# A two-layer transformer block for eight batches: unrolled batches, layer A prepared a batch ahead, the last output units in the turn

## Chip, cores and metric

The kernel runs on one core of one Trainium2 chip. The metric is the device time of one execution in microseconds; times given as the result of a kernel are medians of several executions, times read from a view come from one profiled execution.

## The reference

Eight batches of 512 rows by 128 features go through two layers in float32. `x` is the input.

```python
# layer A, on n = layernorm(x): 16 heads of 8 for q and k, of 32 for v
Q = split_heads(n, 16);  K = split_heads(n @ Wk + bk, 16);  V = split_heads(n @ Wv + bv, 16)
attn = softmax(Q @ K.T + causal mask)
o = (attn @ V) merged to 512 columns
x = x + n + gelu(o) @ Wf + bf
# layer F, on n = layernorm(x): 8 heads of 64, 8 experts for each head
q, k = n @ w_q, n @ w_k;  gates = sigmoid(n @ w_gate)      # (heads, 8)
gm = one_hot(argmax(gates)) * gates
values = einsum('bhne,ehdk,bnd->bhnk', gm, value_experts, n)
out = (softmax(q @ k.T / 8, causal) @ values)
x = x + einsum('bhne,ehkd,bhnk->bhnd', gm, output_experts, out) summed over heads
```

## The kernel before

All batches run through the same program on five engines; each engine's order is written out by hand and semaphores tie them together. `each_batch` (L246) runs `first` (layer A of batch 0), then in a hardware loop seven times `body` (layer F of one batch, then layer A of the next), then `last` (layer F of batch 7). Between them all engines meet (`meet`, L249): each drains, SP clears all semaphores of the batch and lets them go on.

Layer A or F is an `attention` over 4 groups of heads (A: 4 heads each, F: 2), each group in 3 stages of key tiles. For each head a *max unit* makes the scores once for their maxima and softmax denominators (PE `max_unit` L490, DVE `max_unit` L1005, ACT `denominators` L740), `negate` (L1021) makes the offsets, which PE transposes and SP writes as extra rows of the operand by DMA (`maxima_rows`, L323), and a *score unit* makes the scores again with them (PE `score_unit` L518, ACT's exponential L788). POOL cuts the causal triangle (L916) and PE multiplies with the values (`weigh`, L538). Max units of group g + 2 run beside the score units of group g.

Layer A has to be prepared: the transposed, normalised input is split into three bf16 parts for q, and K = n Wk + bk likewise for k (`q_part0` L691, `q_rest` L982, `k_part0` L700 and their neighbours, `transposed` L415, `keys_a` L422). SP writes the parts to DRAM (`parts_to_dram`) and reads them back head by head (`restack_a`, L294), once layer F has let the operands go. All this lies beside layer F's first stages. V is made between F and A: `values_a` on PE (L427, twelve matmuls in banks of `ps_exp`) and on DVE (L1000, with the bias).

Layer F begins with `project_f` (L435): transposes, gates, the projections q and k, then 32 *expert values* (L1190 picks them by the gates). Its result is multiplied with the output experts in 32 *output units*: DVE makes `at` = `osb` * `hots` (L1058), PE adds the product to one bank (`product`, L556). A unit's multiplication waits for the product two before it. `OUTPUTS` (L99) places the 32 units: 8 beside F's last steps, 6 beside A's first max units, 18 beside A's 48 score units. The one-hot rows `hots` come from DRAM by large DMAs on ACT's queue (`repeat_hots`, L722).

I call *turn* what lies between the last score unit of layer A and the expert values of the next layer F: the last `weigh`, `outputs_end` (copy of the sum, transposes, addition, L569, L854, L1061), gelu (L816), `project_back` (L627), the sum `x1` (`first_layer`, L1199), the meeting, then statistics and normalising (L961, L970), transposes, `x_high` (L686) and `x_low` (L976), gates and projections.

Of the kernel before, what the change touches and what calls it, by code (L numbers as in the profile page):

```python
# [11 lines left out]

F32 = mybir.dt.float32
F32R = mybir.dt.float32r
# [26 lines left out]
JUNK = 3  # L41
STEPS = {"A": 4, "F": 3}
# [9 lines left out]
BANK = {("F", "xT", 0): 0, ("F", "gate", 0): 1, ("F", "gmT", 0): 1, ("A", "xT", 0): 0, ("A", "K", 0): 1,  # L52
        ("F", "acc", 0): 1, ("F", "out", 0): 0, ("A", "W", 0): 1}
# [25 lines left out]

def place(phases):  # L80


    at, u = {}, 0
    for phase, steps, first, units in phases:
        at.update({(phase, n): [] for n in range(steps)})
        for m in range(units):
            at[phase, first + m * (steps - first) // units].append(u)
            u += 1
    assert u == T * E
    return at  # L90
# [6 lines left out]


OUTPUTS = place([("F", UNITS["F"], 14, 8), ("pre", STAGES * HG["A"], 0, 6), ("A", UNITS["A"], 0, 18)])  # L99


HOTS_AT = {("F", 1): 0, ("F", 4): 1, ("A", 0): 2, ("A", 4): 3}


def build(nc, x, wk, bk, wv, bv, wf, bf, wq, wkf, wg, ve, oe, ident, consts, out):
    ctx = ExitStack()
    with ctx:
# [3 lines left out]
        sems = []  # L111

        def sem(name):
            sems.append(ctx.enter_context(nc.semaphore(name)))
            return sems[-1]
# [15 lines left out]
        bv_sb = sb("bv_sb", [P, S])  # L131
# [6 lines left out]
        x1 = sb("x1", [P, T, D])  # L138
# [31 lines left out]
        raw = {"wq": at[:, 0], "wkf": at[:, 1], "wg": xn["F"][:, 0, 0:64]}  # L170

        rest = pt[:, 7]

        def part(n):

            return pt[:, (2, 3, 6)[n // 2], :].bitcast(BF16)[:, (n % 2) * S:(n % 2) * S + S]
# [5 lines left out]
        def bank(name):  # L182
# [4 lines left out]
        ps_m = [bank("ps_m0"), bank("ps_m1")] + ps_exp  # L187
# [7 lines left out]

        hot_d = nc.dram_tensor("hot_d", (64, S), BF16).ap()
# [6 lines left out]
        cleared = {n: sem(f"cleared_{n}") for n in ("sp", "pe", "act", "pool", "dve")}  # L203
        y_out = sem("y_out")
        first_of_batch = len(sems)
        arrived = sem("arrived")
        x_in = sem("x_in")
        K2 = lambda n: {k: sem(f"{n}{k}") for k in "AF"}
        ln_st, ln_mv, ln_ve, ln_rs, ln_xn = (K2(n) for n in ("ln_st", "ln_mv", "ln_ve", "ln_rs", "ln_xn"))
        xt_ready, xh_done, xl_done = K2("xt_ready"), K2("xh_done"), K2("xl_done")  # L210
        restacked = sem("restacked")
        restacked_a = [sem(f"restacked_a{g}") for g in range(GROUPS)]
        pair_sent = [sem("pair_sent0"), sem("pair_sent1")]
        max_ready, max_done = K2("max_ready"), K2("max_done")
        neg_step, neg_ready = K2("neg_step"), K2("neg_ready")
        t_ready, t_done = K2("t_ready"), K2("t_done")
        mrow = {k: [sem(f"mrow{k}{n}") for n in range(2)] for k in "AF"}
        s_ready, exp_done = K2("s_ready"), K2("exp_done")
        causal, pv_done = K2("causal"), K2("pv_done")
        den_done, ln_done = K2("den_done"), K2("ln_done")  # L220
        sums_out = K2("sums_out")
        q1, q_r, q2, q3 = sem("q1"), sem("q_r"), sem("q2"), sem("q3")
        k_ready, kf, k1, k_r, k2, k3 = (sem(n) for n in ("k_ready", "kf", "k1", "k_r", "k2", "k3"))
        parts_out = sem("parts_out")
        v_ready, va = sem("v_ready"), sem("va")
        resid = sem("resid")
        gelu_done, w_ready, x1_done = sem("gelu_done"), sem("w_ready"), sem("x1_done")
        gate_ready, gate_exp, gate_step, gt_ready, gmt_done = (
            sem(n) for n in ("gate_ready", "gate_exp", "gate_step", "gt_ready", "gmt_done"))
        gt_made = sem("gt_made")  # L230
        zmax_made, zabs_made, low_gate, soft_made, lng_made = (
            sem(n) for n in ("zmax_made", "zabs_made", "low_gate", "soft_made", "lng_made"))
        qk_ready, qk_hi, qk_lo = sem("qk_ready"), sem("qk_hi"), sem("qk_lo")
# [1053 lines left out]
```

## Time and profile before

| | us |
|---|---|
| median of 3 executions | 1541.37 (1540.88 to 1544.47) |
| profiled execution | 1543.4, of which the span is 1541.3 |
| mean granted clock of TensorE | 0.900 of 2.4 GHz |
| PE busy | 1215.5 us, 79% |
| DVE busy | 907.6 us, 59% |
| ACT busy | 895.6 us, 58% |

The chain that ended last has 41% on PE, 24% on ACT, 14% on DVE and 12% in which an engine waited for nothing that the profile shows. Batch after batch is alike: the sum `x1` (L1204) comes at 129.3, 309.9, 493.2, 677.3 us and so on, every 184 us, and last at 1414.5; the rest, layer F of the last batch, takes 126 us. A busy share of the whole span mixes stages with different limits, so the views below are of single stages of one batch.

### The profile page before, as it was taken

Reading aid. Unit: us, or ns where it says so; the run is one execution under the profiler, and the core shown is the slowest. Engines: PE = TensorE matmul, PEld = TensorE weight load, DVE = VectorE, ACT = ScalarE, POOL = GpSimd, SP = SyncE. Lnnn points to the kernel's source line nnn. Section 1 sums busy time; section 2 is a strip of 40 time slices with the busy share of each in tenths; the row PEclk is TensorE's granted clock in tenths of the full one; section 3 lists DMA queues with packets and bytes.
Section 4 is the critical chain, followed back from the end, with each engine's and each line's share of the span. In section 5 each row is a group of like instructions: output and inputs, shape, how many; then the busy total and the mean of one; then the engine's idle time right before and its main releaser. Section 6 shows DMA issues by size and latency. Waiting matters only on the chain.

```text
span 1541.3 us, 19742 instructions
## 1 busy us (share of the span) xinstructions
PE 1215.5 (79%) x5720; PEld 678.2 (44%) x5720; DVE 907.6 (59%) x2786; ACT 895.6 (58%) x2551; POOL 209.9 (14%) x264
## 2 busy tenths in 40 slices
PE   2667888878886879869789688886888778887978
PEld 1114643356433654337443464335643356434643
DVE  5534747367482756728476474745748276572845
ACT  1773567727594366934678246772668527594351
POOL 2020111201111011110112011120110111111010
PEclk9976989979898889979799798997989979898999
DMA  3312631146220651207421164113632055120722
GB/s 89 102 56 49 148 101 44 36 96 143 74 56 17 132 128 44 56 16 165 107 59 29 42 148 111 47 30 82 140 88 65 8 119 136 57 56 9 162 60 61
DMA packets 64163, 122.18 MB, mean 79 GB/s; under 512 B 13971, under 2 KB 29715, under 8 KB 59683
## 3 DMA queue, kind: packets, MB, share of 16 engines
q1 hardware_dynamic: 58950, 87.77, 23.7%
q10 hardware_dynamic: 5120, 33.56, 9.4%
q14 instruction: 82, 0.67, 0.2%
q8 instruction: 11, 0.18, 0.0%
HBM read 61.37 MB, written 9.06 MB: 46 GB/s over the span
## 4 chain that ended last, share of the span: by engine, by line
PE 41%; ACT 24%; DVE 14%; issue 12%; DMA 3%; SPq 3%; POOL 1%; ACTq 1%; POOLq 1%; DVEq 0%
ACT masked L747 11%; PE ps_m L559 8%; ACT pt L788 7%; PE ps_o L552 6%; DVE masked L1016 4%; PE ps_m L403 4%; PE ps_exp L481 3%; PE ps_m L405 3%; PE ps_m L404 3%; PE ps_m L636 3%; DMA s1q<-zeros_d 3%; PE ps_exp L480 2%; PE ps_exp L482 2%; PE ps_max L480 2%; DVE pt L1168 2%
## 5 line engine op out<-in xcount | busy, mean ns | idle before, releaser
L1016 DVE CUSTOM_DVE_ANT_0 masked<-ps_max,mask 128x512 f32<-128x512 f32 (+3 forms) x768 | 352.0, 485 | 228.8 <-PE ps_max L480 152.2
L747 ACT ACTIVATE masked<-masked,low 128x512 f32<-128x512 f32 (+3 forms) x768 | 427.6, 560 | 76.7 <-DVE low L1016 74.3
L788 ACT ACTIVATE pt<-ps_exp 128x384 f32<-128x384 f32 (+1 forms) x576 | 293.7, 523 | 188.3 <-PE ps_exp L482 134.5
L559 PE MATMUL ps_m<-at,oe_sb 128*128 128x512 f32 x512 | 268.6, 611 | 5.6 <-DVE at L1058 3.5
L916 POOL TENSOR_SCALAR_AFFINE_SELECT pt<-pt 128x512 f32<-128x512 f32 (+2 forms) x192 | 133.3, 694 | 800.0 <-ACT pt L788 800.0
L1058 DVE TENSOR_TENSOR at<-osb,hots 128x512 f32<-128x512 f32 x256 | 180.7, 708 | 75.7 <-PE ps_m L559 75.7
L552 PE MATMUL ps_o<-pt,val 128*32 128x128 f32 (+6 forms) x1536 | 191.1, 473 | 11.2 <-POOL pt L916 11.2
L480 PE MATMUL ps_exp<-s1q,s2k 96*128 96x128 bf16 (+3 forms) x512 | 133.5, 319 | 64.6 <-ACT pt L788 53.1
L480 PE MATMUL ps_max<-s2k,s1q 96*128 96x512 bf16 (+3 forms) x512 | 141.4, 326 | 52.6 <-DMA s1q<-zeros_d 39.5
L747 ACT ACTIVATION_READ_ACCUMULATOR masked<-masked,low 128x1 f32 x768 | 151.5, 197 | 0.0
L480 PEld LDWEIGHTS ps_exp<-s1q,s2k 96*128 96x128 bf16 x512 | 43.2, 99 | 226.3 <-ACT pt L788 174.3
L481 PE MATMUL ps_exp<-s1q,s1k 128*128 128x256 f32 (+2 forms) x256 | 108.9, 436 | 34.9 <-DMA s2q<-mt_f 19.0
L480 PEld LDWEIGHTS ps_max<-s2k,s1q 96*128 96x128 bf16 x512 | 49.6, 101 | 133.2 <-issue 48.0
L1190 DVE COPY_PREDICATED val<-osb,ps_exp 128x512 f32<-128x512 uint32 x128 | 92.7, 734 | 19.8 <-PE ps_exp L405 19.8
L559 PEld LDWEIGHTS ps_m<-at,oe_sb 128*128 128x128 f32 x512 | 86.5, 193 | 39.9 <-DVE at L1058 33.1
L481 PEld LDWEIGHTS ps_exp<-s1q,s1k 128*128 128x128 f32 x256 | 54.1, 211 | 89.8 <-issue 54.2
L552 PEld LDWEIGHTS ps_o<-pt,val 128*32 128x32 f32 (+1 forms) x1536 | 54.5, 123 | 88.8 <-issue 55.6
L482 PE MATMUL ps_exp<-s2q,s2k 96*128 96x256 f32 (+2 forms) x256 | 89.5, 360 | 0.0
L481 PE MATMUL ps_max<-s1k,s1q 128*128 128x256 f32 (+2 forms) x256 | 87.2, 350 | 2.8 <-DVE low L1016 2.8
L482 PE MATMUL ps_max<-s2k,s2q 96*128 96x256 f32 (+2 forms) x256 | 85.3, 342 | 0.0
L836 ACT ACTIVATE pt<-ps_m 128x512 fp32r<-128x512 f32 x64 | 38.3, 598 | 75.5 <-PE ps_m L405 74.7
L924 POOL TENSOR_TENSOR val<-val,gmax 128x512 f32<-128x512 f32 x32 | 32.7, 1043 | 334.3 <-DVE val L1190 334.3
(144 smaller groups left out, 1679.9 us busy)
## 6 DMA issues: line engine op xcount, KB each, us to landing
hots<-hot_d ACTq DMA_DIRECT2D x64, 512.0 KB, 5.6
s1q<-pt SPq DMA_DIRECT2D x128, 128.0 KB, 2.4
s1k<-pt SPq DMA_DIRECT2D x128, 128.0 KB, 2.4
s2k<-parts_k SPq DMA_DIRECT2D x96, 96.0 KB
s1q<-parts_q SPq DMA_DIRECT2D x96, 96.0 KB
s2q<-pt SPq DMA_DIRECT2D x64, 128.0 KB, 2.4
s2k<-pt SPq DMA_DIRECT2D x64, 128.0 KB, 2.4
parts_q<-pt SPq DMA_DIRECT2D x24, 128.0 KB, 2.4
```

The source lines that it names most:

```text
L403: mm(dst, lh, rh, start=True, stop=False)
L480: return mm(dst, l1[0:KROWS, h, l2], r1[0:KROWS, h, r2], start=True, stop=True)
L481: mm(dst, l1[0][:, h, l2], r1[0][:, h, r2], start=True, stop=False)
L482: return mm(dst, l1[1][0:KROWS, h, l2], r1[1][0:KROWS, h, r2], start=False, stop=True)
L552: last = mm(ps_o[g % 2][j * w:j * w + w, qt * P:S], val[:, kt, h * w:h * w + w], pt[:, (n % 2) * 4 + j, c0:c1], start=kt == 0, stop=kt == 3)
L559: mm(ps_m[1][:], oe_sb[:, u], at[:, u % 2], start=u == 0, stop=u == T * E - 1).then_inc(at_used, 1)
L747: last = nc.scalar.activation(e, e, ACT.Exp, bias=low[:, g % 2, c:c + 1], scale=-1.0, accum_out=den[:, g % 2, c:c + 1])
L788: nc.scalar.activation(pt[:, (n % 2) * 4 + j, 0:c1 - c0], ps_exp[u % 2][:, c0:c1], ACT.Exp).then_inc(exp_done[k], 1)
L916: nc.gpsimd.affine_select(out=v, in_=v, compare_op=ALU.is_ge, fill=0.0, base=0, pattern=[[0, HG[k]], [0, m], [1, P]], channel_multiplier=- ...
L1016: last = v.tensor_tensor_reduce(out=masked[:, u % JUNK, c0:c0 + w], in0=src[:, c0:c0 + w], in1=mask[:, S - w:S], scale=-1.0, scalar=POS, o ...
L1058: v.tensor_tensor(at[:, u % 2], osb[:, u // E], hots[:, u // E % 2, u % E], ALU.mult).then_inc(at_done, 1)
L1190: v.copy_predicated(val[:, t].rearrange("p (h k) -> p h k", k=64), pick, ps_m[BANK[("F", "moe1", n)]][:].rearrange("p (h k) -> p h k", k=6 ...
```

## The change

1. Semaphores are no longer cleared. Each has a count per batch (`Tally`), waits are for `per * batch + n`, and `for b in range(B)` is unrolled in Python: no meetings, no hardware loop.
2. Layer A of batch b + 1 is prepared in the second half of layer A of batch b (`PREP`: steps 24 to 37), no longer beside layer F. Its V is made in the turn, copied by ACT, written to DRAM (`v_d`) by SP, and read back after layer F. The bias of V moves to the copy of the weighed sums and to gelu.
3. `TURN = 8`: 8 of the 32 output units leave layer A's score steps and stand in the turn. Layer A's other 10 stand in its first 36 steps. The units' multiplication is on VectorE, as before.
4. Some tiles change place: the gates, the transposed output and `project_back` have banks of `ps_max`, the parts lie in `masked`, `x1` and the residual have two buffers, gelu writes the last group to a tile of its own.

```diff
-OUTPUTS = place([("F", UNITS["F"], 14, 8), ("pre", STAGES * HG["A"], 0, 6), ("A", UNITS["A"], 0, 18)])
+TURN = E
+OUTPUTS = place([("F", UNITS["F"], 14, 8), ("pre", STAGES * HG["A"], 0, 6), ("A", 3 * STAGES * HG["A"], 0, 10)])
+PREP = {"stats": 24, "norm": 26, "xT": 28, "q0": 29, "q_rest": 30, "q1": 31, "q2": 32, "K": 32, "k0": 34, "k_rest": 35,
+        "k1": 36, "k2": 37}
...
# SP
+            def layer_a(a):
+                if a + 1 < B:
+                    sp.wait_ge(resid.sem, resid.count(a, 2))
+                    sp.dma_start(x_sb[:], x[a + 1].rearrange("(t p) d -> p t d", p=P)).then_inc(x_in.sem, 16)
+                for g in range(GROUPS):
+                    maxima_rows("A", a, g)
...
+                if a + 1 < B:
+                    parts_to_dram(a + 1, "q")
+                    parts_to_dram(a + 1, "k")
+                    for t in range(T):
+                        sp.wait_ge(va.sem, va.count(a + 1, t + 1))
+                        sp.dma_start(v_d[t], val[:, t]).then_inc(v_out[t].sem, 16)
...
+            def layer_f(f):
+                restack_f(f)
+                for g in range(3):
+                    maxima_rows("F", f, g)
...
+                for g in range(GROUPS):
+                    if g == 2:
+                        maxima_rows("F", f, 3)
+
+                    sp.wait_ge(s_ready["F"].sem, s_ready["F"].count(f, (g + 1) * STAGES * HG["F"]))
+                    restack_a(g)
+                sp.wait_ge(pv_done["F"].sem, pv_done["F"].count(f, NST))
+                for t in range(T):
+                    sp.wait_ge(v_out[t].sem, v_out[t].count(f, 16))
+                    sp.dma_start(val[:, t], v_d[t]).then_inc(v_back.sem, 16)
...
# PE
+            def turn(a):
+
+                f, first = a - 1, T * E - TURN
+                if a + 1 < B:
+                    pe.wait_ge(exp_done["A"].sem, exp_done["A"].count(a, UNITS["A"]))
+                    values_a(a + 1, (0, 1))
+                if f >= 0:
+                    product(f, first - 1)
+                    product(f, first)
+                project_back(a, (0, 1, 2))
+                if f >= 0:
+                    product(f, first + 1)
+                    product(f, first + 2)
+                project_back(a, (3,))
+                if a + 1 < B:
+                    values_a(a + 1, (2, 3))
+                if f >= 0:
+                    for u in range(first + 3, T * E - 1):
+                        product(f, u)
+                transposed("F", a)
+                if f >= 0:
+                    product(f, T * E - 1)
...
+                if n == 0 and k == "A" and b > 0:
+                    if v_back.count(b - 1, 16 * T):
+                        pe.wait_ge(v_back.sem, v_back.count(b - 1, 16 * T))
...
# ACT
+            def turn(a):
+
+                g = GROUPS - 1
+                act.wait_ge(sums_out["A"].sem, sums_out["A"].count(a, g))
+                nc.scalar.activation(osb[:, 0:g], osb[:, 0:g], ACT.Gelu).then_inc(gelu_done.sem, 1)
+                if a + 1 < B:
+                    values_a(a + 1, (0, 1))
+                act.wait_ge(pv_done["A"].sem, pv_done["A"].count(a, NST))
+                if a + 1 < B:
+                    act.wait_ge(parts_out.sem, parts_out.count(a + 1, 16 * WRITES))
+                for t in range(T):
+                    c = slice(t * P, (t + 1) * P)
+                    nc.scalar.activation(osb3[:, c], ps_o[g % 2][:, c], ACT.Gelu, bias=bv_sb[:, g:g + 1]
+                                         ).then_inc(gelu_done.sem, 1)
+                nc.scalar.preload_act_table_set(EXP_LN)
+                if a + 1 < B:
+                    values_a(a + 1, (2, 3))
+                x_high("F", a)
+                if a > 0:
+                    outputs_end(a - 1)
...
# DVE
+            def experts(f):
+                dve.wait_ge(x1_done.sem, x1_done.count(f, 1))
+                statistics("F", f, x1[f % 2])
+                normalise("F", f, x1[f % 2])
+                if f > 0:
+                    for u in range(T * E - TURN + 3, T * E - 1):
+                        choose(f - 1, u)
+                x_low("F", f)
+                if f > 0:
+                    for u in range(T * E - 1, T * E):
+                        choose(f - 1, u)
...
+                    if u == 0 and f > 0:
+                        outputs_end(f - 1)
...
+            for b in range(B):
+                attention_a(b)
+                if b > 0:
+                    for u in range(first, first + 3):
+                        choose(b - 1, u)
+                first_layer(b)
+                experts(b)
+                attention_f(b)
```

`choose` is the multiplication of a unit (L1058), with the wait for the product two before it as it was.

## Rows read from the trace of the kernel before

**Rows 1.** Page of before, part 1: busy us (share of the span) and instructions.

```profile
PE 1215.5 (79%) x5720; PEld 678.2 (44%) x5720; DVE 907.6 (59%) x2786; ACT 895.6 (58%) x2551; POOL 209.9 (14%) x264
```

**Rows 2.** Stretches: length, busy us (count) of each engine, granted clock, DMA share, GB/s.

```profile
552.00:573.40 21.40, 19.06 (x93) 12.99 (x93) 11.09 (x44) 16.70 (x50) 2.96 (x6) 0.89 0.62 147
616.20:646.90 30.70, 25.30 (x138) 9.33 (x136) 24.00 (x89) 29.70 (x100) 4.48 (x6) 1.00 0.31 70
646.90:665.05 18.15, 17.40 (x111) 6.53 (x111) 6.26 (x13) 13.47 (x32) 4.79 (x6) 1.00 0.01 2
```

**Rows 3.** Timeline, the turn: last exponentials, last weigh, gelu, project_back twice.

```profile
480.08 0.87 ACT L788 ACTIVATE pt<-ps_exp 128x384 f32<-128x384 f32 x2 [0.32 <-PE ps_exp L480]
482.17 0.86 PE L552 MATMUL ps_o<-pt,val 128*32 128x256 f32 x16 [1.18 <-POOL pt L916]
486.03 1.48 ACT L820 ACTIVATE osb<-osb 128x1536 f32<-128x1536 f32 x1
487.66 5.44 PE L636 MATMUL ps_m<-wf_sb,osb 128*128 128x128 f32 x32 [2.17 <-ACT osb L820]
305.94 3.81 PE L636 MATMUL ps_m<-wf_sb,osb 128*128 128x128 f32 x32 [2.17 <-ACT osb L820]
```

**Rows 4.** Timeline, start of layer F: transposes, gates, first low part, expert values.

```profile
500.70 1.25 PE L419 MATMUL ps_m<-ident_sb,xnF 128*128 128x128 f32 x4 [7.60 <-DVE xnF L973]
503.36 0.42 PE L403 MATMUL ps_m<-wg_h,xh 128*128 128x64 f32 x1 [1.41 <-DVE xl L978]
508.23 0.69 DVE L1168 SCALAR_TENSOR_TENSOR pt<-ps_m,pt 128x512 fp32r<-128x512 f32 x1 [1.43 <-ACT pt L836]
513.76 0.50 PE L403 MATMUL ps_m<-ve_h,xh 128*128 128x512 f32 x1 [0.40 <-DVE pt L1168]
```

**Rows 5.** Timeline, VectorE at the barrier: start us, us, instruction [idle before <-releaser].

```profile
493.19 0.69 DVE L1204 TENSOR_TENSOR x<-ps_m,x_sb 128x512 f32<-128x512 f32 x1 [6.97 <-PE ps_m L636]
497.81 0.87 DVE L963 BATCH_NORM_STATS2 st<-x 128x6 f32<-128x128 f32 x4 [3.92 <-issue]
1415.97 0.87 DVE L963 BATCH_NORM_STATS2 st<-x 128x6 f32<-128x128 f32 x4 [0.81 <-SPq L255]
```

**Rows 6.** Timeline, start of layer A: V matmuls, logarithm, first step of negate.

```profile
602.34 0.39 PE L404 MATMUL ps_exp<-wv_h,xl 128*128 128x512 f32 x1
602.57 0.40 PE L405 MATMUL ps_exp<-wv_l,xh 128*128 128x512 f32 x1
603.34 0.22 ACT L759 ACTIVATE lnd<-den 128x16 f32<-128x16 f32 x1
606.07 0.16 DVE L1029 TENSOR_TENSOR nm_r<-low,lnd 128x16 f32<-128x16 f32 x1
```

**Rows 7.** Timeline, layer F's first groups: third batch (551 to 568), last batch.

```profile
551.92 0.77 PE L481 MATMUL ps_exp<-s1q,s1k 128*128 128x512 f32 x1 [2.00 <-issue]
568.30 0.68 SPq L332 DMA_DIRECT2D s2q<-mt_f  x1
1470.06 0.77 PE L481 MATMUL ps_exp<-s1q,s1k 128*128 128x512 f32 x1 [4.30 <-DMA s2q<-mt_f]
1481.88 0.47 PE L481 MATMUL ps_exp<-s1q,s1k 128*128 128x512 f32 x1 [1.57 <-issue]
1487.60 1.29 SPq L332 DMA_DIRECT2D s2q<-mt_f  x2
```

**Rows 8.** Timeline, PE in layer A's second half: a product, then scores.

```profile
660.44 1.02 PE L559 MATMUL ps_m<-at,oe_sb 128*128 128x512 f32 x2
661.30 0.33 PE L480 MATMUL ps_exp<-s1q,s2k 96*128 96x384 bf16 x1
```

**Rows 9.** Stretches of 1 us around the start of layer F's attention, third batch.

```profile
550.00:551.00 1.00, 0.00 (x0) 0.00 (x0) 0.00 (x0) 1.00 (x3) 0.79 (x1) 0.50 0.02 4
556.00:557.00 1.00, 1.00 (x5) 0.81 (x4) 0.90 (x8) 0.68 (x3) 0.00 (x0) 0.60 0.93 254
```

**Rows 10.** Stretch: second half of layer A's scoring in the first batch.

```profile
104.00:121.40 17.40, 15.68 (x72) 3.75 (x76) 0.00 (x0) 9.54 (x22) 3.13 (x4) 0.50 0.34 122
```

More of the change, by code:

```diff
@@ L679, in _ @@
-            each_batch("pe", pe, first, body, last)
+                if groups[-1] == GROUPS - 1:
+                    last.then_inc(w_ready.sem, 1)
+            def turn(a):
[19 more added lines that the diff above has]
+                    product(f, T * E - 1)
@@ L682, in _ @@
+            for u in range(E - 1, T * E):
+                product(B - 1, u)
+            outputs_end(B - 1)
         @block.scalar
@@ L773, in attention @@
[L773 to L774 removed]
+                        act.wait_ge(sent.sem, sent.count(b, 2 * 16 * SENDS))
                 for g in range(GROUPS):
[L776 removed]
+                    if g == SPLIT_AT and k == "A" and b == 0:
                         expert_weights_high()
@@ new lines, in experts, with outputs_end @@
+                        act.wait_ge(zabs_made.sem, zabs_made.count(f, 1))
+                        nc.scalar.activation(zabs[:], zabs[:], ACT.Exp, scale=-1.0).then_inc(soft_made.sem, 1)
+                        act.wait_ge(soft_made.sem, soft_made.count(f, 1))
+                        nc.scalar.activation(zabs[:], zabs[:], ACT.Ln, bias=1.0).then_inc(soft_made.sem, 1)
+            def outputs_end(f):
+                act.wait_ge(at_used.sem, at_used.count(f, T * E))
+                copy(at[:, 0], ps_m[BANK[("F", "acc", 0)]][:]).then_inc(acc_copied.sem, 1)
@@ L878, in body @@
[L878 to L891 removed]
+                    copy(dst[:], raw[name]).then_inc(split_hi.sem, 1)
@@ L894, in _ @@
+            act.wait_ge(w_in[1].sem, w_in[1].count(0, 16 * 3))
+            for b in range(B):
+                attention("A", b)
+                turn(b)
+                experts(b)
+                attention("F", b)
+            repeat_hots(B - 1, 2)
+            repeat_hots(B - 1, 3)
+            outputs_end(B - 1)
         @block.gpsimd
@@ L957, in _ @@
+            pool.wait_ge(w_in[1].sem, w_in[1].count(0, 16 * 3))
+            residual(0)
+            for b in range(B):
+                attention("A", b)
+                inverse_deviation("F", b)
+                gated_values(b)
+                attention("F", b)
+                if b + 1 < B:
+                    residual(b + 1)
         @block.vector
@@ L1256, in _ @@
-            each_batch("dve", dve, first, body, last)
+            v.memset(nm_f[:], 0.0).then_inc(set_v.sem, 1)
+            v.memset(mask[:], 0.0).then_inc(set_v.sem, 1)
+            for e in range(E):
+                v.memset(rank[:, e:e + 1], float(E - e))
+            v.memset(s1q[:].bitcast(F32), 0.0).then_inc(set_v.sem, 1)
+            dve.wait_ge(x_in.sem, x_in.count(0, 16))
+            statistics("A", 0, x_sb)
+            normalise("A", 0, x_sb)
+            dve.wait_ge(w_in[0].sem, w_in[0].count(0, 16 * 4))
@@ L1259 @@
+            for u in range(E, T * E):
+                choose(B - 1, u)
+            outputs_end(B - 1)
 _NAMES = ["x", "wk", "bk", "wv", "bv", "wf", "bf", "wq", "wkf", "wg", "ve", "oe", "ident", "consts"]
```

1236 lines of the change are left out of this document (601 added, 635 removed).

## The prediction, made before the changed kernel was run

> **What bounds the kernel now.** I read the page first: PE is busy 79% of the span and no engine is full [rows 1], so one share of busy time decides nothing and each stage has to be asked for its own limit. Then the table of stretches of one batch [rows 2]. In the first half of layer A's scoring ACT is busy 29.70 of 30.70 us: ACT-bound. In the second half PE is busy 17.40 of 18.15 us and ACT 13.47: there the products of the output units pace it. Last the timelines of the turn, from the last exponential of layer A to the first expert values of layer F. I call the end of that last exponential X; it is at 480.95 (480.08 + 0.87) [rows 3], and the expert values begin at 513.76 [rows 4], X + 32.8 us. In the turn each engine waits for the next one; what is put into the chain there costs its full length, and what is put beside it costs nothing. That decides this change.
>
> **Barrier.** All engines meet eight times; six times the loop goes back behind the meeting. There the sum that gives x1 ends at 493.88 and the statistics start at 497.81: 3.92 us. The meeting that falls through takes 0.81 us (the idle time that the row of 1415.97 gives) [rows 5]. So the barrier with its jump gives back 6 x 3.92 + 2 x 0.81 = 25.1 us, if nothing takes its place. The Trainium skill ("Runtime: NRT & Kernel Launch", Instruction fetch mechanics) says that a taken branch breaks the sequential prefetch; the 3.1 us between the two kinds of meeting agree.
>
> **V leaves the start of layer A.** Now twelve V matmuls run there, VectorE adds the bias, and `negate` starts at 606.07 although the logarithm that it needs ended at 603.56; the stretch behind is carried by VectorE [rows 6]. After, `negate` comes first, so the stretch starts 2.4 us earlier, 7 x -2.4 = -16.8. Between 0 (something else is late) and 3.3 us (all twelve matmuls). V's way back from DRAM is needed only in the first `weigh` of layer A; its loads are issued behind the last restack, on SP's queue, some 10 us before.
>
> **Preparation leaves layer F.** This looks like 3.6 us of ACT (six copies of 0.6 us) in a busy stretch. But the trace holds that stretch without preparation: the last batch has none. From the first score of F to the DMA issue of the third group of maxima it takes 568.30 - 551.92 = 16.4 us with preparation and 1487.60 - 1470.06 = 17.5 us without [rows 7]. In the last batch PE stands idle 1.57 us ahead of the first score of the second group (1481.88) [rows 7]: it waits for rows of maxima that travel while the hots are being repeated. The Trainium skill ("Trainium Kernel Development and Optimization", Key Constraints) says that DMAs of SP's and ACT's queues run on the same 16 DMA engines and interleave; this row fits. Everything behind it in F hangs on that chain. So I take +0.5 us a batch, 7 x 0.5 = +3.5; bounds -2.2 (copies count, PE then limits) and +1.1 (the last batch exactly).
>
> **Preparation enters the second half of layer A.** Outputs there fall from 9 to 3; a product costs PE 0.86 us (660.44 to 661.30) [rows 8], so PE loses 5.2 us and gains four transposes and three matmuls, some 1.4 us. ACT gains 3.6 us: 13.47 + 3.6 = 17.1, plus the stalls between stages while `weigh` holds back the next scores (0.7 us each in two or three stages): 18.65 against 18.15. PE's gain is thus turned into an ACT bound: +0.5 x 6 = +3. The last batch has no preparation: -1.2. Bounds: -1 to +1.5 a batch. DVE, with no maxima left there, hides its 6 us.
>
> **The turn, step by step (times after X).** Before: last `weigh` at +1.2, `outputs_end` and the table load ahead of gelu, gelu at +5.1, `project_back` from +6.7 to +12.2, x1 done at +12.9 [rows 3, 5]. After: `weigh` +1.2 to +2.05; V0 and V1, 6 x 0.235 us (spacing of the V matmuls) [rows 6], to +3.6; products 23 and 24 to +5.3; `project_back` for three groups at the fast rate (3.81 us for 32, the row with its clock up) [rows 3] to +8.2; products 25 and 26 to +9.95; the last group to +10.95; x1 at +11.7. Gelu takes 1.48 us [rows 3]; with a table load that I put at about as much it is ready by +3, no longer behind the copy. So -1.2 us, with 4 products and half of V inside. V2 and V3 fill PE to +12.4. Then statistics, POOL's power and the normalising: x1 to the first transpose took 497.81 to 500.70, 2.9 us [rows 4, 5], but in PE's queue the transposes stand behind products 27 to 30, and in DVE's queue the four multiplications stand behind the normalising, which ends at +15.35. Each multiplication waits for the product two before it. So product 27 starts at +16.05, four in a row on PE follow, and only then the transposes, x_high, x_low (2.6 us from 500.70 to 503.36) [rows 4], then multiplication 31 and product 31 ahead of the gates, 1.5 us more.
>
> How long that takes hangs on PE's clock. PE has nothing from +12.4 to +16.05. A short idle stretch at the end of the expert values says what follows: after an idle stretch that begins in 547 and is broken by 0.66 us of transposes, the granted clock is 0.50 (1.2 GHz) in 550 to 551 with PE idle; work that restarts at 551.92 runs at 0.50 until about 556.6, and 556 to 557 has a mean of 0.60 [rows 7, 9]. So product 27 starts at half clock (1.71 us each), the clock is back about 4.7 us later, the transposes start at +21.85 and the gates at +25.3, where they now start at 503.36, X + 22.4. With the clock up the gates and the first projection take 3.6 us rather than 508.23 - 503.36 = 4.87 [rows 4]; the new 0.69 us addition in `outputs_end` goes into DVE's chain behind. Expert values at X + 35.2 against 32.8: +2.4 us, although the barrier's 3.9 us are gone. Six such turns: +14.4. The last loses only 0.8 us of barrier and has no V: +3.9. Bounds for a turn: 0 (the clock stays up: gates at +23.1) and +6.2 (half clock throughout).
>
> **First batch.** Its second half runs at half clock, PE 15.68 of 17.40 us busy [rows 10]; transposes and K cost PE 2.6 us there, V0 and V1 stand ahead of `project_back` (2.6 us at half clock), less 0.8 us of barrier and a little clock: +3.8. Bounds 0 and +5.
>
> **Sum.** -16.8 + 3.5 + 3.0 - 1.2 + 14.4 + 3.9 + 3.8 = +10.6 us. The profiled execution took 1543.4 us (span 1541.3), 2 us over the median 1541.4; the sum gives 1554 for it and 1552 for the median.
>
> **Rivals.** (1) The forecast: the barrier's time goes to the chain of products in the turn. Chance 0.38.
> (2) PE's clock stays up in the turn, because V2 and V3 come late enough: 7 x -2.3 = -16, giving 1536. For it: no wait of PE is over 4 us. Against: the clock fell some 2.4 us after PE went quiet in the row above. Chance 0.22.
> (3) F does gain from losing the preparation, 2.2 us a batch instead of +0.5: -19, giving 1533. For it: ACT is busy 16.70 of 21.40 us there [rows 2]. Against: the last batch. Chance 0.18; together with (2) 1517, within this chance.
> (4) The other side, beyond the forecast: the clock is down for the whole turn, or falls again while ACT and DVE make xh and xl. 1.1 to 3.8 us more per turn, 1560 to 1579; it decides once PE is idle for over 2 us twice in the turn. Chance 0.15.
> (5) The change doesn't do what it says: V's writes or loads are late and layer F's base copies (which wait for `v_out`) or the first `weigh` take the place. The writes of V0 and V1 are issued near X + 4, and the base copies come near X + 33, so little speaks for it. 1545 to 1560, chance 0.07.
>
> **Range and chances.** About what a measurement can tell from no change is 0.3%, 4.6 us. The likeliest case's own range is 1543 to 1563 (F and the second half of A at their bounds). The 8-in-10 range reaches to the fast cases on one side and to half of (4) on the other: 1522 to 1570. Faster 0.34, mostly (2) and (3); same 0.18; slower 0.48, from (1), (4) and (5).
>
> **What would show it.** Right: in the turn, x1 done near X + 11.7; PE idle some 3.7 us, then products 27 to 30 ahead of the transposes; gates near X + 25; the granted clock at half as product 27 starts. `negate` within 0.2 us of the logarithm at the start of A. The second half of A about 18.6 us with ACT near full. F's second group still waiting for its maxima rows. Wrong: transposes within 4 us of x1, or F's first two groups over 1.5 us shorter, or a granted clock of 1.0 through the turn.

## The result, and the profile after

The changed kernel takes 1574.93 us (median of 4 executions, 1570.59 to 1577.83), the kernel before beside it 1541.9: ratio 1.0209, interval 1.0181 to 1.0237. Forecast were 1552 and a range of 1522 to 1570: the sign came out, the size did not, and the time lies above the range. The profiled execution took 1570.6 us, span 1568.9 against 1541.3: +27.6 us where the sum of the prediction says +10.6. It is the fastest of the four; the median is 4 us above it. All steps below are of profiled executions, one for each kernel. The ratios of all tables leave out slow executions, one of the kernel before (1973.49 us) and one of e1 (1563.04 us; the median of its other nine is 1551.3).

The page of after, PE's busy time and its granted clock over 40 slices:

```profile
PE 1233.9 (79%) x5720; PEld 665.2 (42%) x5720; DVE 889.1 (57%) x2754; ACT 921.7 (59%) x2583; POOL 208.9 (13%) x264
PEclk8568989889898989989799897988989899899999
...
PE 45%; ACT 18%; DVE 16%; issue 12%; DMA 4%; SPq 3%; POOL 2%; ACTq 0%; DVEq 0%; POOLq 0%
```

PE does the same 5720 matmuls in 18 us more [rows 1]: more of them run at the lower clock. I divided every batch of both traces at the same marks and summed the differences by the terms of the prediction. X is again the end of layer A's last exponential; the second half of A here is the stretch from the end of its last max unit to X.

| term | forecast, us | measured, us |
|---|---|---|
| start of A without V, 7 batches | -16.8 | -16.7 |
| first half of A, 7 batches | 0 | +7.0 |
| second half of A, batches 2 to 7 | +3.0 | +21.8 |
| second half of A, last batch | -1.2 | -0.6 |
| turn, X to expert values, batches 2 to 7 | +14.4 | +12.0 |
| last turn | +3.9 | +2.3 |
| first batch up to its expert values | +3.8 | +0.2 |
| layer F from the expert values on, 8 batches | +3.5 | +1.6 |
| sum | +10.6 | +27.6 |

Six of eight terms are within 4 us. The miss is the second half of layer A, and a smaller one in its first half, where I had put nothing.

**The second half of A.** Stretches of after in the columns of [rows 2] (length, then busy us and count of PE, its weight loads, DVE, ACT and POOL, then granted clock, DMA share, GB/s): the one that answers to 646.90:665.05 there, in the third batch and in the last one, which prepares nothing; then three single microseconds:

```profile
465.27:487.09 21.82, 17.53 (x104) 5.64 (x106) 8.57 (x19) 16.68 (x38) 5.87 (x7) 0.83 0.13 38
1410.38:1427.89 17.51, 13.67 (x101) 4.32 (x99) 2.87 (x8) 13.78 (x32) 4.25 (x6) 1.00 0.01 2
479.00:480.00 1.00, 0.83 (x9) 0.38 (x13) 1.00 (x2) 1.00 (x3) 0.00 (x0) 0.93 0.13 36
480.00:481.00 1.00, 1.00 (x14) 0.35 (x6) 0.07 (x1) 0.46 (x2) 0.68 (x1) 0.50 0.60 167
490.00:491.00 1.00, 1.00 (x5) 0.83 (x6) 0.00 (x0) 0.04 (x1) 0.00 (x0) 0.95 0.00 0
```

It takes 21.82 us for 18.15; I had forecast 18.65. Neither PE (17.53) nor ACT (16.68) fills it. The granted clock falls to 0.50 (1.2 of 2.4 GHz) just before 480 and is back a little after 490, so the last 7 us of the stretch and the first 3 of the turn run at half clock. Timeline of PE and ACT, two lines from ahead of the fall, three from behind it:

```profile
477.67 0.88 PE L478 MATMUL ps_exp<-s1q,s2k 96*128 96x512 bf16 x2 [0.56 <-ACT pt L863]
479.17 0.39 PE L478 MATMUL ps_exp<-s1q,s2k 96*128 96x512 bf16 x1 [0.62 <-ACT pt L863]
484.54 0.82 PE L478 MATMUL ps_exp<-s1q,s2k 96*128 96x256 bf16 x4
485.13 0.87 ACT L863 ACTIVATE pt<-ps_exp 128x384 f32<-128x384 f32 x2 [1.87 <-PE ps_exp L478]
485.68 0.88 PE L478 MATMUL ps_exp<-s1q,s2k 96*128 96x256 bf16 x4 [0.32 <-ACT pt L863]
```

Ahead of the fall PE waits again and again for an exponential, each time for under 1 us. At half clock ACT waits 1.87 us for scores, then PE for ACT: each waits for the other in turn.

**The turn.** Timeline, third batch, X = 487.09:

```profile
491.40 1.88 PE L576 MATMUL ps_m<-at,oe_sb 128*128 128x512 f32 x4
498.60 0.69 DVE L1310 TENSOR_TENSOR x<-ps_max,x 128x512 f32<-128x512 f32 x1 [4.59 <-PE ps_max L670]
502.85 1.28 DVE L1147 TENSOR_TENSOR at<-osb,hots 128x512 f32<-128x512 f32 x2
503.58 5.56 PE L576 MATMUL ps_m<-at,oe_sb 128*128 128x512 f32 x8 [3.64 <-DVE at L1147]
508.98 0.60 PE L418 MATMUL ps_m<-ident_sb,xnF 128*128 128x128 f32 x4
512.15 0.59 PE L401 MATMUL ps_max<-wg_h,xh 128*128 128x64 f32 x1
521.86 0.79 PE L401 MATMUL ps_m<-ve_h,xh 128*128 128x512 f32 x1
```

and a stretch from just behind the start of product 27:

```profile
503.80:507.20 3.40, 3.40 (x5) 1.29 (x5) 1.02 (x2) 0.00 (x0) 0.00 (x0) 0.50 0.00 0
```

x1 is done at X + 12.2 (forecast 11.7), PE idles 3.64 us (3.7), product 27 starts at X + 16.5 (16.05) and runs at half clock (granted clock 0.50 in that stretch), the transposes start at X + 21.9 (21.85), the gates at X + 25.1 (25.3), the expert values at X + 34.8 (35.2).

**Layer F.** Its first score stands as far behind the expert values as before, 38.4 us for 38.2. With the preparation gone PE comes there earlier and waits longer for the rows of maxima, 4.30 us for the 2.00 of [rows 7]; so it is in all eight batches (4.3 to 4.7 us), as in the last batch of before:

```profile
560.27 0.77 PE L479 MATMUL ps_exp<-s1q,s1k 128*128 128x512 f32 x1 [4.30 <-DMA s2q<-mt_f]
```

### The profile page after: what moved, and what is told of

It is laid out like the page before. It is cut to its first block, busy times and chain, and to the rows that moved or that the text cites. A ratio compares the mean times of both kernels' runs of the same rounds, so it can differ in the third digit from the quotient of the medians.

```text
span 1568.9 us, 19785 instructions
## 1 busy us (share of the span) xinstructions
PE 1233.9 (79%) x5720; PEld 665.2 (42%) x5720; DVE 889.1 (57%) x2754; ACT 921.7 (59%) x2583; POOL 208.9 (13%) x264
## 4 chain that ended last, share of the span: by engine, by line
PE 45%; ACT 18%; DVE 16%; issue 12%; DMA 4%; SPq 3%; POOL 2%; ACTq 0%; DVEq 0%; POOLq 0%
PE ps_m L576 9%; ACT masked L805 8%; PE ps_o L567 7%; ACT pt L863 7%; DVE masked L1102 5%; PE ps_exp L479 3%; PE ps_m L401 3%; PE ps_exp L478 3%; DMA s1q<-zeros_d 2%; PE ps_m L403 2%; PE ps_m L402 2%; PE ps_exp L480 2%; DVE at L1147 2%; PE ps_max L670 2%; PE ps_exp L401 2%
## 5 line engine op out<-in xcount | busy, mean ns | idle before, releaser
L576 PE MATMUL ps_m<-at,oe_sb 128*128 128x512 f32 x512 | 279.7, 647 | 46.3 <-DVE at L1147 44.1
L1147 DVE TENSOR_TENSOR at<-osb,hots 128x512 f32<-128x512 f32 x256 | 176.0, 690 | 125.8 <-PE ps_m L576 125.8
L478 PE MATMUL ps_exp<-s1q,s2k 96*128 96x128 bf16 (+3 forms) x512 | 142.8, 338 | 97.8 <-ACT pt L863 84.1
L567 PE MATMUL ps_o<-pt,val 128*32 128x128 f32 (+6 forms) x1536 | 206.3, 516 | 6.5 <-POOL pt L994 6.5
L576 PEld LDWEIGHTS ps_m<-at,oe_sb 128*128 128x128 f32 x512 | 91.8, 202 | 109.1 <-DVE at L1147 90.0
```

The costliest lines, as they stand in the source:

```text
L478: return mm(dst, l1[0:KROWS, h, l2], r1[0:KROWS, h, r2], start=True, stop=True)
L567: last = mm(ps_o[g % 2][j * w:j * w + w, qt * P:S], val[:, kt, h * w:h * w + w], pt[:, (n % 2) * 4 + j, c0:c1], start=kt == 0, stop=kt == 3)
L576: mm(ps_m[1][:], oe_sb[:, u], at[:, u % 2], start=u == 0, stop=u == T * E - 1).then_inc(at_used.sem, 1)
L1147: v.tensor_tensor(at[:, u % 2], osb[:, u // E], hots[:, u // E % 2, u % E], ALU.mult).then_inc(at_done.sem, 1)
```

## The experiments

The theory after the first comparison has two parts. *Chain*: products 27 to 30 hold the transposes up. *Second half of A*: the copies on ACT, the falling clock, or both. "Turn" below is X to the expert values, "second half" from the last max unit to X, both of the third batch.

| kernel | us | ratio to before, interval | turn | second half |
|---|---|---|---|---|
| before | 1541.9 to 1543.6 | | 32.8 | 19.7 |
| changed | 1574.93 | 1.0209 (1.0181 to 1.0237) | 34.8 | 23.35 |
| e1, four units in the turn | 1552.4 | 1.0044 (1.0015 to 1.0072) | 31.8 | 23.7 |
| e2, turn in another order | 1524.93 | 0.9900 (0.9878 to 0.9922) | 28.0 | 23.2 |
| e3, three copies on VectorE | 1553.12 | 1.0074 (1.0055 to 1.0093) | 34.2 | 20.85 |
| e4, before, loop written out | 1522.68 | 0.9878 (0.9860 to 0.9895) | 29.5 | 19.7 |
| e5, six copies on VectorE | 1548.8 | 1.0035 (1.0015 to 1.0055) | 33.3 | 20.7 |
| e6, e2 and e3 | 1502.49 | 0.9751 (0.9728 to 0.9773) | 27.0 | 20.9 |
| e7, filler in the second half | 1580.38 | 1.0241 (1.0195 to 1.0287) | 34.2 | 22.5 |
| e8, no unit in the turn | 1501.8 | 0.9738 (0.9721 to 0.9754) | 24.7 | 22.4 |
| e9, e8 and e3 | 1505.07 | 0.9737 (0.9699 to 0.9775) | 24.6 | 22.2 |
| e10, e8 and e5 | 1497.68 | 0.9704 (0.9680 to 0.9727) | 25.2 | 22.0 |
| e11, e10 and filler at A's start | 1496.24 | 0.9703 (0.9687 to 0.9720) | 25.0 | 22.0 |
| e12, e10 again, beside e11 | 1505.63 | 0.9751 (0.9730 to 0.9772) | 25.2 | 22.0 |

**e1, four units in the turn.**

```diff
-TURN = E
+TURN = 4
-... ("A", 3 * STAGES * HG["A"], 0, 10)
+... ("A", 3 * STAGES * HG["A"], 0, 14)
```

> The changed kernel with TURN = 4: four output units instead of eight in the turn, 14 instead of 10 in the first 36 score steps of layer A. Nothing stands between the sum x1 and the transposes of layer F any more. Theory 'chain' (the four products 27 to 30 cost the turn what they hold up): from x1 to the first transpose 2.9 us instead of 9.6, seven times, so about -46 us, less 0 to 3.4 us a batch for four more products beside the scores: 1532 to 1552 against 1575. Rival 'work' (PE's work is only moved, and the clock falls wherever it lies): 1562 to 1575.

The median, 1552.4 (executions from 1538 to 1563), is at the upper end of the theory's range and 10 us below the rival's. The first part came as expected, x1 to the first transpose 3.0 us for 9.6. But only 3.0 of the 6.7 us stay in the turn: its stretch, beside those of the changed kernel and of e8:

```profile
492.95:524.73 31.78, 24.92 (x110) 16.61 (x103) 11.61 (x30) 11.23 (x18) 2.10 (x2) 0.76 0.13 46
```

```profile
487.09:521.86 34.77, 26.48 (x119) 15.96 (x111) 14.20 (x34) 10.85 (x18) 2.11 (x2) 0.84 0.12 42
```

```profile
479.66:504.39 24.73, 17.59 (x98) 13.41 (x94) 9.62 (x27) 11.13 (x18) 2.11 (x2) 0.86 0.17 59
```

With four units (the first of the three) the mean clock of the turn is 0.76, lower than with eight (0.84): gates to expert values take 11.4 us, with eight 9.7. The way to the gates is shorter, and what follows it is slow.

**e2, the turn in another order.**

```diff
 # PE
-                if a + 1 < B:
-                    values_a(a + 1, (2, 3))
-                if f >= 0:
-                    for u in range(first + 3, T * E - 1):
-                        product(f, u)
-                transposed("F", a)
-                if f >= 0:
-                    product(f, T * E - 1)
+                if f >= 0:
+                    product(f, first + 3)
+                    product(f, first + 4)
+                if a + 1 < B:
+                    values_a(a + 1, (2, 3))
+                if f >= 0:
+                    product(f, first + 5)
+                transposed("F", a)
+                if f >= 0:
+                    product(f, first + 6)
 # and product 31 behind the gates; DVE: 27 and 28 ahead of first_layer
                 statistics("F", f, x1[f % 2])
+                choose(f - 1, T * E - 3)
                 normalise("F", f, x1[f % 2])
+                choose(f - 1, T * E - 2)
                 x_low("F", f)
```

> The changed kernel with all eight units still in the turn, in another order: the multiplications 27 and 28 stand ahead of the sum x1, 29 behind the statistics, 30 behind the normalising, 31 behind x_low; product 29 stands ahead of the transposes, 30 behind them, 31 behind the gates. Theory 'chain': the same work fills PE's wait, x1 to first transpose falls from 9.6 to 3.5 to 4.5 us and the clock has no long idle stretch to fall in: about 6 us a turn, 7 turns, 1530 to 1540. Rival 'clock': the clock is down by then whatever the order, the products run at half speed ahead of and behind the transposes: only 2 to 3 us a turn, 1554 to 1562.

1524.93: 50 us less than the changed kernel, 5 us below the expected range. Timeline, third batch, X = 478.47:

```profile
489.93 1.88 PE L578 MATMUL ps_m<-at,oe_sb 128*128 128x512 f32 x4
490.13 0.69 DVE L1315 TENSOR_TENSOR x<-ps_max,x 128x512 f32<-128x512 f32 x1 [0.20 <-PE ps_max L672]
493.06 1.02 PE L578 MATMUL ps_m<-at,oe_sb 128*128 128x512 f32 x2
494.20 1.01 PE L418 MATMUL ps_m<-ident_sb,xnF 128*128 128x128 f32 x4
496.62 0.30 PE L401 MATMUL ps_max<-wg_h,xh 128*128 128x64 f32 x1
```

The same eight products. 27 and 28 run while DVE makes x1, 29 while it normalises, and the transposes start 3.4 us behind x1 instead of 9.7. The granted clock of this turn is 0.93. The second half of A keeps its 23.2 us, so the two losses are two places.

**e3, three of the preparation's copies on VectorE.**

```diff
-                copy(part(1), rest).then_inc(q2.sem, 1)          # ACT, and so for parts 3 and 4
+                v.tensor_copy(part(1), rest).then_inc(q2.sem, 1)  # DVE
```

> The changed kernel with three of the six preparation copies of layer A (q1, k0, k1: SBUF to SBUF, 0.63 us each) on VectorE, which is busy 10.1 of 23.3 us there, instead of ScalarE. Theory 'ACT in the chain' (a copy on ACT delays the next exponential and with it PE's next scores by its whole length, though ACT is busy only 18.2 of 23.35 us): 3 x 0.63 x 6 to 7 batches = -11 to -13 us, 1562 to 1564. Rival 'clock' (the second half of A is longer because TensorE's clock falls in it): no change, or 1570 to 1580.

1553.12, 22 us less where 11 to 13 were expected, and the second half fell by 2.5 us a batch, more than the 1.9 us that the three copies take. The clock, which should not have moved, is at 1.00 in the whole stretch now. Which of the two the 2.5 us belong to, e7 and e9 tell.

**e5, all six copies on VectorE.** The other three (two from PSUM, one with the bias) go as well; no line but theirs changes.

> The changed kernel with all six preparation copies of layer A on VectorE, none on ScalarE. With three of them moved the second half of A fell by 2.4 us a batch. Theory 'ACT in the chain': the other three (1.9 us) go too, the second half comes to that of the last batch, which has no preparation (19.0 us): -4.3 against the changed kernel's 23.3, -26 in all, and the clock is up there as in the last batch: 1542 to 1550. Rival 'clock and order' (what is left is PE's: transposes and K in the queue of the scores, and a wait for the now longer chain on VectorE): no more than the -2.4 of three copies, 1553 to 1560.

The total fits the theory (1548.8), the stretch does not: 20.7 us, 0.2 less than with three, where 19.0 was forecast. There the rival holds: 1.6 us of the preparation (20.68 against the 19.05 of the last batch of after) is left with nothing of it on ACT.

**e7, needless products in the second half.**

```diff
                             score_unit("A", a, g, s, j)
+                            if u == 28:
+                                pe.wait_ge(max_done["A"].sem, max_done["A"].count(a, UNITS["A"]))
+                            if u >= 28:
+                                mm(ps_max[0][:], ident_b[:], mask[:], start=True, stop=True)
```

> The changed kernel with one needless product of 128 x 512 in bf16 (about 0.2 us, its result is never read) behind each of the last 20 score units of layer A; ScalarE has its copies as before. Theory 'the clock falls because PE does too little there': the clock stays up, 1 to 2.5 us a batch are won back although PE does 4 us more: 1555 to 1568. Rival 'the clock is not the cause, PE's order is': 20 x 0.2 us lie in the chain of the scores, 0 to +4 us a batch: 1575 to 1600.

The stretches that answer to 465.27:487.09 and 1410.38:1427.89 of after, in e7, and to the first of them in e3 and in e8:

```profile
460.96:481.95 20.99, 18.54 (x126) 6.81 (x126) 8.56 (x19) 16.68 (x38) 5.86 (x7) 1.00 0.14 39
1413.45:1432.20 18.75, 17.15 (x119) 5.93 (x119) 2.86 (x8) 13.76 (x32) 4.22 (x6) 1.00 0.01 2
```

```profile
465.10:484.42 19.32, 15.16 (x108) 5.28 (x106) 11.10 (x22) 15.11 (x35) 5.98 (x7) 1.00 0.15 43
```

```profile
458.82:479.66 20.84, 18.90 (x118) 7.47 (x118) 11.90 (x26) 16.70 (x38) 5.60 (x7) 1.00 0.14 40
```

In e7 ACT's busy time is to 0.01 us that of the changed kernel, 20 matmuls are added, and the stretch is shorter, 20.99 for 21.82: the clock is 1.00 in place of 0.83. In the last batch, where the clock was up anyway, the same 20 matmuls cost 18.75 - 17.51 = 1.2 us. If they cost as much beside the preparation, the fall costs 0.8 + 1.2 = 2.1 us a batch here (before rounding), and 0.6 to 1.0 us in the turn behind (x1 at X + 11.4 for 12.0 to 12.4). The kernel as a whole is no faster, 1580.4, and the total of the theory (1555 to 1568) was wrong. In the profiled executions the second halves of A give back 3.5 us together in batches 2 to 8, but the turns take 3.6 us more (in most the transposes come 0.8 us later behind x1, and two turns have 16 us at half clock for 7) and layer F, which the edit does not touch, takes 8.0 us more. Why layer F does was not found.

**e8, no unit in the turn.** All 18 stand beside the 48 score units again, only the last product in the turn.

```diff
-TURN = E
+TURN = 0
-... ("A", 3 * STAGES * HG["A"], 0, 10)
+... ("A", UNITS["A"], 0, 18)
```

> The changed kernel with no output unit in the turn but the last product: 18 beside the 48 score steps of layer A as before the change. With four units in the turn x1 to the first transpose fell by 6.6 us, and 2 to 4 us came back behind it at half clock (gates to expert values +2.2). Theory: the rest of the turn falls by the 2 x 1.9 us of products 23 to 26 less what their multiplications and the half clock cost, and the second half of A grows by up to 1.2 us: 1545 to 1555, no better than with four. Rival (every product taken out of the turn is won): 1530 to 1540.

1501.8: 73 us less than the changed kernel, below both expectations. The turn is 10.0 us shorter. And the second half of A, with nine products for three (of the eight, two went to the first half), is not longer but 1.0 us shorter (the last of the stretches above: PE 18.90 of 20.84 us busy, clock 1.00). Timeline of the turn, X = 479.66:

```profile
484.02 2.84 PE L670 MATMUL ps_max<-wf_sb,osb 128*128 128x128 f32 x24
487.79 0.69 DVE L1295 TENSOR_TENSOR x<-ps_max,x 128x512 f32<-128x512 f32 x1 [10.98 <-PE ps_max L670]
491.49 1.00 PE L418 MATMUL ps_m<-ident_sb,xnF 128*128 128x128 f32 x4 [2.34 <-DVE xnF L1031]
493.91 0.30 PE L401 MATMUL ps_max<-wg_h,xh 128*128 128x64 f32 x1 [1.41 <-DVE xl L1036]
504.39 0.72 PE L401 MATMUL ps_m<-ve_h,xh 128*128 128x512 f32 x1 [0.42 <-DVE pt L1255]
```

x1 at X + 8.8 (before: 12.9), gates at X + 14.3 (22.4). This is what the rest of the change brings; the eight units took all of it back. Of the 70.8 us between the profiled executions of the changed kernel and of e8, 64.9 lie in the seven turns, 4.8 in the second halves of A and 5.7 in the first; the first batch and layer F are 4.7 longer.

**e6, e2 and e3 together.**

> The changed kernel with both edits, the turn in the new order and three copies on VectorE. If the two losses are separate places, they add: 1525 - 17 to 22 = 1503 to 1508. Rival (the clock: what keeps PE busier in one place lets the clock fall in another): 1515 or more.

1502.49: they add. With the clock up at X the turn is 27.0 us, 2.3 more than with no unit in it: filling it well is nearly as good as emptying it.

**e9 and e10, no unit in the turn and three or six copies on VectorE.**

> The changed kernel with no output unit in the turn and three of layer A's six preparation copies on VectorE. With the clock up throughout the second half of A (as it is with all 18 units beside the scores) the copies can only give what they take themselves. Theory 'the casts were worth a clock fall, not their own time': the second half goes from 22.37 to 21.4 to 21.9 us, so 3 to 6 us in all: 1495 to 1500. Rival 'the casts cost their own length': -2.4 us a batch again, 1483 to 1489.

> As the run before, with all six copies on VectorE, which also multiplies the 18 units there. Theory: 0 to 1 us a batch less than with three, 1490 to 1499. Rival (VectorE's queue becomes the bound: the units' multiplications stand behind waits for transposes and K): slower than with three by 1 to 2 us a batch, 1502 to 1510.

The second half of A goes from 22.37 to 22.21 and to 22.02. The same edit that gave 2.5 us a batch in e3 gives 0.16: where the clock is up already, the copies' own time is nearly free. Theory "a clock fall, not their own time" holds, more strongly than it was put. The stretch here has nine products, though, in e3 three; there, at full clock, the three copies are worth about 0.4 us (an estimate: 22.52 - 1.23 for the filler in e7, against 20.85 in e3). As totals, 1505.07 (1496 to 1508) and 1497.68 differ little from e8's 1501.8, and e9 is above its range. The profiled execution of e9 is 7.8 us longer than that of e8: its first halves of A take 4.9 us more, with a fall of the clock in four of seven batches where e8 has none, and layer F takes 7.3 us more, for which no cause was found; other places are shorter.

**e4, the kernel before with its loop written out.**

```diff
-            with eng.Fori(0, B - 1) as i:
+            for i in range(B - 1):
                 body(i)
                 meet()
```

> The kernel before with its hardware loop written out, the meetings of all engines kept: only the jump back goes. Theory of the prediction (the jump costs 3.92 - 0.81 = 3.1 us, six times): -18.7 us, 1523. Rival 'cold code' (the instructions of each batch are fetched anew either way): within 3 us of 1541.

1522.68, the forecast to 0.3 us; against the runs beside it the gain is 20.9 us, not 18.7. VectorE at the meeting of e4:

```profile
490.90 0.69 DVE L1204 TENSOR_TENSOR x<-ps_m,x_sb 128x512 f32<-128x512 f32 x1 [6.97 <-PE ps_m L636]
492.26 0.87 DVE L963 BATCH_NORM_STATS2 st<-x 128x6 f32<-128x128 f32 x4 [0.66 <-SPq L255]
```

0.66 us in place of the 3.92 of [rows 5]. That one line puts the old kernel 52 us below the changed one, and it is half of what e8 gains (1543.39 - 1501.8 = 41.6 us).

**e11 and e12, the wait at the start of A.** The first half of A is 39.5 us in most batches, but 42.3 in two of after. What stands there: a timeline of after, whose third line has the wait, and the stretch that follows it:

```profile
612.18 0.22 ACT L820 ACTIVATE lnd<-den 128x16 f32<-128x16 f32 x1
612.48 0.17 DVE L1115 TENSOR_TENSOR nm_r<-low,lnd 128x16 f32<-128x16 f32 x1 [2.84 <-issue]
614.20 0.34 PE L478 MATMUL ps_max<-s2k,s1q 96*128 96x384 bf16 x1 [1.94 <-DVE low L1102]
```

```profile
616.30:619.70 3.40, 3.28 (x7) 1.39 (x7) 2.41 (x10) 2.43 (x10) 0.00 (x0) 0.51 0.89 268
```

`negate` follows the logarithm at once, as forecast. But PE, with no V to make, waits 1.94 us, and the clock falls 2 us later. Before, with the V matmuls ahead of it, the wait was 1.1 us:

```profile
607.77 0.34 PE L480 MATMUL ps_max<-s2k,s1q 96*128 96x384 bf16 x1 [1.09 <-DVE low L1016]
```

e11 puts work that nobody needs into the wait:

```diff
                     for n in range(n_units):
+                        if a > 0 and n == 2:
+                            pe.wait_ge(exp_done["F"].sem, exp_done["F"].count(a, 0))
+                            for _ in range(8):
+                                mm(ps_exp[0][:], ident_b[:], mask[:], start=True, stop=True)
                         max_unit("A", a, g, n)
```

> The kernel with no unit in the turn and all preparation copies on VectorE, with eight needless products of 128 x 512 in bf16 (0.2 us each, never read) on PE at the start of layer A, ahead of the third max unit, where PE waits 1.94 us since V was taken away from there; they lie inside that wait. In the profile without them TensorE's clock falls to half some 2.5 us after that wait in five of seven batches, 1.2 us each. Theory 'the twelve V matmuls had covered this wait': no fall there, the first half of A is 39.5 us in every batch, 5 to 10 us less than the run beside it. Rival 'the fall has another cause, or the needless products only add': within 3 us of the run beside it, or slower by up to 7 x 0.5 us.

> The same kernel without the needless products, on the same chip: no unit in the turn, all preparation copies on VectorE. It was 1497.7 before; 1494 to 1501 expected.

1496.24 against 1505.63 side by side, -9.4 us. The wait in e12, and in e11:

```profile
418.15 0.34 PE L478 MATMUL ps_max<-s2k,s1q 96*128 96x384 bf16 x1 [1.94 <-DVE low L1080]
```

```profile
414.41 1.67 PE L603 MATMUL ps_exp<-mask,ident_b 128*128 128x512 bf16 x7
416.29 0.34 PE L478 MATMUL ps_max<-s2k,s1q 96*128 96x384 bf16 x1 [0.21 <-DVE low L1084]
```

In e11 the row shows seven of the eight filling matmuls, and the wait is gone. In e12 the first half of A has a fall in five of seven batches (40.6 to 41.8 us); in e11 all seven take 39.5 to 39.6. The two kernels' profiles differ by 8.8 us there, out of 12.5. e12 is the kernel of e10, which took 1497.7 in other runs: so far the same program differs from one set of runs to the next, and only runs side by side compare. By its ratio e11 (0.9703) is level with e10 (0.9704), both 3.0% under the kernel before.

Over all profiles of this study the fall behind this wait shows 30 times in 77 batches: 1.2 to 2.4 us behind a wait of 1.94 us (2.29 in a few), in the eleven kernels without V and without filler there. It shows in none of the 14 batches of before and e4, with a wait of 1.1 us, and in none of the seven of e11. But e6 and e8 have the wait in all seven batches and no such fall, so the wait alone does not make it.

## Why the prediction was right, and where it was wrong

**Barrier: right.** 3.1 us for each jump was to give 18.7 us; e4 shows 20.9 against the runs beside it (1543.57), and 20.3 from span to span (1541.3 to 1521.0).

**V leaves the start of A: right in its size, incomplete.** -2.4 us a batch came in every batch. The forecast put nothing for what PE's twelve matmuls did there: they kept a wait short (1.1 us for 1.94). Without them the clock falls behind it in some batches; in the changed kernel's profile two of seven, 5.6 of the 7.0 us. The other 1.4 are 0.2 us in every batch, without a fall. That the wait brings the fall is shown by e11 against e12; in the changed kernel itself the filler was not tried.

**F: right in that nothing is gained, not in the wait.** The rival in which F gains 2.2 us a batch did not come; from the expert values on it changed by +1.6 us in eight batches, where +3.5 was forecast. Layer F, which no edit touches, took 739 to 751 us in the profiles of the changed kernel and e1 to e3 and e5 to e12, so +1.6 can't be told from +3.5. The prediction put it on the second group: its row says "issue" for the 1.57 us, not the maxima, and in after only the third batch has such a wait there (1.50 us). What holds F is the wait of the first group, 4.3 us.

**The turn: right, step by step,** with each of the marks above within 0.5 us, the half clock at product 27 included; and the reading that what is put into the chain costs its full length is what e2 and e8 show (28.0 and 24.7 us for 34.8). The rival "the clock stays up in the turn" did not happen in the changed kernel; in e6, at a clock of 0.98, the turn takes 27.0 us. In the first batch V0 and V1 were to cost 2.6 us; its turn is 1.6 us shorter, its second half 2.0 us longer, and the whole came to +0.2 for +3.8.

**The second half of A: the step that failed.** I compared sums of busy time, 17.1 us for ACT and some 13.6 for PE, added two stalls, and said that PE's gain turns into an ACT bound, +0.5 us. ACT's sum was near (16.68), but ACT stood idle for 5.1 of the 21.82 us: it did not bound the stretch. The runs show three terms, of the stretch that was 19.68 us:

- six products fewer: -0.63 us (last batch, 19.05), not the 5.2 us that PE saves. PE was busy 17.40 of 18.15 us [rows 2] and is busy 13.67 of 17.51 in the last batch: what it saves it waits. In e8 six products more cost 0.8 us in the last batch (19.85).
- the preparation at full clock: +2.2 us, an estimate. In e7 the stretch is 22.52 with 1.23 us of it for the filler, so 21.3 without, against 19.05. Only 0.6 us of it is the copies' place on ACT (e5: 20.7); 1.6 us are left with all of them on VectorE. With the six products fewer I had +0.5 net.
- the falling clock: +2.1 us (e7), and 0.6 to 1.0 us more in the turn behind. I had watched PE's idle time in the turn and not in the stretch that I had just emptied. Emptying alone does not bring the fall, though: the last batch has lost the same six products and stays at 1.00.

-0.6 + 2.2 + 2.1 = +3.7, and +3.5 to +3.9 were measured; the three terms are parts of one stretch of the third batch, so their sum is no test of them. e3 gives a second way to the fall: it took it away without filler and gained 2.5 us; less 0.16 for its three copies (e9) that leaves 2.3 us, near the 2.1. Six batches are +21.8 instead of +3.0; with the first half's 7.0 and the other terms together 8.8 us under their forecast, that is the whole difference between +10.6 and +27.6. So the terms that were too high hid a third of the miss. The medians differ by 33.0 us, 5.4 more than the two profiled executions. That was not traced execution by execution; that more falls of the clock make it is only argued (the executions' mean granted clock goes from 0.888 in the fastest to 0.881 in the slowest, but not in order: 0.884 at 1573.69 us, 0.886 at 1576.16).

The range was too narrow because its ends for the second half of A, -1 to +1.5 us a batch, came from the same busy sums. A fall of the clock there was in none of the five cases. That 1575 lies within the 1560 to 1579 of rival (4) is luck: (4) has the falls in the turn, and the six turns came out 2.4 us under the forecast together. The 1543 us given for the likeliest case's lower end holds with the second half of A alone; F's own lower bound would bring it to 1524.

What exactly makes up the 1.6 us of preparation that stay with all copies on VectorE (transposes and K in PE's queue ahead of the scores, or the bank that they share with the maxima) was not separated.

## What to carry to other kernels

Where two engines feed each other through two banks, products in the waits of the one for the other are nearly free (six of them 0.8 us in the last batch). Moved out of there and into a serial chain they pay full price: eight units a batch, 65 us in seven turns and 73 in all. Before taking work from an engine, ask what else that work did: filling a wait of PE can hold its clock up. And count each edit alone; this change held a gain of some 40 us (e8), half of it from the jump alone (e4), and a loss of 73.

## What the runs showed of the hardware

What TensorE does ahead of a fall of its clock can differ little from what it does where the clock stays up. The first 16.1 us behind the last max unit, in after (third batch, where the clock falls at the end of them, and last batch, where it stays at 1.00) and in e3 (third batch, stays):

```profile
463.74:479.84 16.10, 12.11 (x78) 4.51 (x78) 9.84 (x29) 13.80 (x34) 5.18 (x5) 1.00 0.13 35
1408.85:1424.95 16.10, 12.34 (x87) 4.16 (x87) 3.48 (x10) 13.25 (x33) 4.24 (x5) 1.00 0.01 2
```

```profile
463.57:479.67 16.10, 12.82 (x88) 4.78 (x84) 11.51 (x31) 12.83 (x32) 5.44 (x6) 1.00 0.12 35
```

PE is busy 12.11 us where the fall comes, 12.34 and 12.82 where it does not; its longest wait is 0.94 us in all three. The fall comes 15.9 to 16.3 us behind the last max unit in each of batches 2 to 7 of after. Over the whole stretch PE looks busier there, 17.53 of 21.82 us (80%) for 13.67 of 17.51 (78%), because its last 7 us run at half clock. At the start of A a wait of 1.94 us was followed by a fall in some batches and not in others of the same execution (e12: five of seven), though the waits are alike to 0.01 us. The Trainium skill ("TensorE: Matmul & The Clock Gate", HAM oscillation — how this bites in real kernels) says that in a matmul kernel that waits for DMAs between its groups of matmuls the clock goes down again and again. The traces agree that it goes down again and again, with 309 us of the kernel before and 352 us of the changed one at half clock, but the waits ahead of the two falls followed here are for ScalarE and VectorE.

Matmuls whose result nobody reads can pay. Eight of 0.2 us in a wait of 1.94 us took 9.4 us off the whole kernel (e11 against e12), while 20 of them in a stretch of many waits under 1 us kept the clock up there and left the whole no faster (e7).

Moving three copies of 0.63 us from ScalarE to VectorE gave 2.5 us a batch where a fall of the clock went with it (e3) and 0.16 us where the clock was up already and PE had six more products in the stretch (e9): one edit, two prices.
